# A decoder kernel in which rounded fp32 halves give way to plain fp32 products, and the experts' second products move behind the next first ones

## What is computed

```python
for l in range(4):
    h = rmsnorm(x, sg[l])
    x = attn_block(h, h, sWq[l], sWk[l], sWv[l], sWo[l], sbo[l], pe_q, pe_q, mask) + x
    h = rmsnorm(x, cg[l])
    x = attn_block(h, chunked_seq, cWq[l], cWk[l], cWv[l], cWo[l], cbo[l], pe_q, pe_k, None) + x
    h = rmsnorm(x, fg[l])
    x = gelu(h @ fW1[l] + fb1[l]) @ fW2[l] + fb2[l] + x
# attn_block: 8 heads of 64, rotary embedding of q and k, softmax(q k^T) v, @ Wo
h = relu(einsum('bth,ehf->betf', x, W1) + b1);  y = einsum('betf,efh->beth', h, W2)   # MoE
y = silu(xf @ wg[e].T) * (xf @ wu[e].T) @ w_down[e].T                                 # GLU
```

## Time and profile before

| | us |
|---|---|
| median of three runs | 1341.22 (1340.53 to 1349.2) |
| span of the profiled execution, first to last instruction | 1334.7 |
| median of the runs less this span | 6.5 |
| PE busy | 1161.6 (87%) |
| DVE, ACT, POOL busy | 779.1, 706.8, 554.6 |

### The profile page before, as it was taken

One profiled execution on the slowest core, in us unless ns is written; L12 is line 12 of the kernel. 1 busy time (PEld: TensorE's weight loads), 2 busy tenths in 40 slices (PEclk: granted clock), 3 DMA queues, 4 the chain that ended last, 5 costly groups with the idle time before them and its releaser, 6 DMA issues.

```text
span 1334.7 us, 21229 instructions
## 1 busy us (share of the span) xinstructions
PE 1161.6 (87%) x7374; PEld 766.2 (57%) x7374; DVE 779.1 (58%) x2164; ACT 706.8 (53%) x1889; POOL 554.6 (42%) x643
## 2 busy tenths in 40 slices
PE   4399998979999897999988899988669976897898
PEld 2255564655556566565556555555559964454687
DVE  7766655476665557666555766565352235775455
ACT  2177665547766536767543776655144433563332
POOL 2467543467754347766236677433221010111110
PEclk8699999999999999999999999999879988998899
DMA  4001010001111000200100020100111100000010
GB/s 139 16 10 17 17 40 9 25 1 39 25 17 41 25 1 1 47 17 17 41 25 1 1 49 17 33 1 1 48 52 33 49 0 1 1 1 1 9 36 26
DMA packets 60857, 31.00 MB, mean 23 GB/s; under 512 B 34260, under 2 KB 52049, under 8 KB 60753
## 3 DMA queue, kind: packets, MB, share of 16 engines
q1 hardware_dynamic: 60753, 29.64, 8.6%
HBM read 28.47 MB, written 1.16 MB: 22 GB/s over the span
## 4 chain that ended last, share of the span: by engine, by line
PE 69%; DVE 13%; POOL 6%; DMA 6%; ACT 4%; issue 2%; SPq 0%; POOLq 0%; DVEq 0%
PE bank L1644 11%; PE bank L1598 7%; PE bank L1704 7%; PE bank L1621 7%; PE bank L1861 4%; DMA dram_r<-recs 4%; PE bank L2081 3%; PE bank L1672 3%; PE bank L1792 3%; PE bank L1794 2%; PE bank L1793 2%; PE bank L1655 2%; PE bank L1590 2%; DMA recT<-dram_r 2%; PE bank L1675 1%
## 5 line engine op out<-in xcount | busy, mean ns | idle before, releaser
L937 DVE CUSTOM_DVE_ANT_0 bank<-bank,maskrow 128x512 f32<-128x512 f32 x256 | 172.1, 715 | 96.2 <-PE bank L1598 95.0
L1343 ACT ACTIVATE probs<-bank,tops 128x512 f32<-128x512 f32 x256 | 174.3, 685 | 99.0 <-DVE tops L937 98.3
L1355 ACT ACTIVATE KA<-bank 128x512 f32<-128x512 f32 x256 | 139.0, 600 | 25.2 <-PE bank L1621 20.5
L1598 PE MATMUL bank<-QR 64*128 64x512 f32 x768 | 126.1, 436 | 16.7 <-DVE rot L926 12.1
L1621 PEld LDWEIGHTS bank<-ident,probs 128*128 128x128 f32 x1024 | 117.0, 141 | 38.6 <-issue 26.3
L1644 PE MATMUL bank<-KA,Vs 128*64 128x512 f32 x512 | 135.4, 615 | 3.9 <-DVE AT L960 3.9
L1621 PE MATMUL bank<-ident,probs 128*128 128x128 f32 x1024 | 134.3, 274 | 2.3 <-ACT Vs L1315 2.3
L1339 ACT ACTIVATE probs<-bank,tops 128x154 f32<-128x154 f32 x256 | 96.5, 387 | 67.9 <-DVE tops L934 66.8
L925 DVE TENSOR_TENSOR rot<-bank,cos 128x512 f32<-128x512 f32 (+1 forms) x112 | 73.5, 656 | 63.8 <-PE bank L1675 54.6
L1598 PEld LDWEIGHTS bank<-QR 64*128 64x128 f32 x768 | 65.2, 189 | 44.2 <-issue 24.2
L703 POOL TENSOR_TENSOR rot<-rot,sin 128x512 f32<-128x512 f32 x48 | 61.2, 1276 | 61.9 <-DVE rot L926 61.9
(11 more groups left out here) (274 smaller groups left out, 2545.8 us busy)
## 6 DMA issues: line engine op xcount, KB each, us to landing
recT<-dram_r SPq DMA_DIRECT2D x56, 128.0 KB, 3.3
W<-in_W SPq DMA_DIRECT2D x8, 256.0 KB, 3.1
Vc<-in_wup SPq DMA_DIRECT2D x8, 192.0 KB, 2.4
W<-in_sWk SPq DMA_DIRECT2D x4, 256.0 KB, 4.2
W<-in_sWq SPq DMA_DIRECT2D x4, 256.0 KB, 4.4
W<-in_sWv SPq DMA_DIRECT2D x4, 256.0 KB, 4.7
wo<-in_sWo SPq DMA_DIRECT2D x4, 256.0 KB, 3.8
ck<-in_cWk SPq DMA_DIRECT2D x4, 256.0 KB, 2.8
```

The costliest lines, as they stand in the source:

```text
L937: v.tensor_tensor_reduce(bank[i][:, :], bank[i][:, :], maskrow[:, u.b * S:(u.b + 1) * S], -SCALE, 3.0e38, ALU.add, ALU.min, tops[:, g % 4, ...
L1343: c.activation(to, bank[i][:, :], ACT.Exp, bias=tops[:, g % 4, e, 0:1], scale=-1.0, accum_out=sums[:, n, e, k:k + 1]).then_inc(q.probs_rea ...
L1355: c.activation(turned_self(u)[:, half, :, k * P:(k + 1) * P], bank[4 + half][:, :].rearrange("p (c t) -> p c t", t=P), ACT.Copy).then_inc( ...
L1598: ins = mm(bank[first + e][:, :], QH[rows_of(e), u.j, a, w], KH[rows_of(e), u.j, c, :], start=(n == 0), stop=(n == 2))
```

## The change

All halves go. The five weight matrices are used as loaded, the input is `hT` alone, rotated keys and queries are one tile each (`rope_sum` in place of `rope_halves` and `rope_alone`), and each former triple is one plain fp32 product. The copies and subtractions on ACT, DVE and POOL go with them, also the store of x to DRAM and its reload, which had made room for halves. In both expert blocks the second products of b = 1 come behind the first products of b = 0 of the next expert, and the weights of the first and of the second product have loads and semaphores of their own. The diff, cut:

```diff
-                    for n, (a, c) in enumerate(((0, 0), (0, 1), (1, 0))):
-                        for e in range(2):
-                            ins = mm(bank[first + e][:, :], QH[rows_of(e), u.j, a, w], KH[rows_of(e), u.j, c, :],
-                                     start=(n == 0), stop=(n == 2))
+                    for e in range(2):
+                        mm(bank[first + e][:, :], QT[rows_of(e), u.j, c0:c0 + P], KT[rows_of(e), u.j, u.b * S:(u.b + 1) * S],
+                           start=True, stop=True).then_inc(q.scores_full, 1)
...
-                mm(bank[i][:, :], whigh[name][:, w], inh[:, S0], start=True, stop=False)
-                mm(bank[i][:, :], wlow[name][:, w], inh[:, S0], start=False, stop=False)
-                pe.wait_ge(q.low_ready, low_at[b])
-                return mm(bank[i][:, :], whigh[name][:, w], inl[:, S0], start=False, stop=True)
+                return mm(bank[i][:, :], whole[name][:, w], hT[:, S0], start=True, stop=True)
...
-                    lend([i], q.low_ready)
-                    input_at[b], low_at[b] = see.next(q.hT_ready), see.now(q.low_ready)
+                    lend([i], q.hT_ready)
+                    input_at[b] = see.now(q.hT_ready)
...
-                elif p.what in ("k", "q") and p.b == 0 and p.j < 2:
-                    rope_alone()
                 elif p.what == "k":
-                    rope_halves(KH[:, p.j, :, :])
-                elif p.what == "q":
-                    rope_halves(QH[:, p.j, :, :])
-                elif p.what == "cq":
+                    rope_sum(KT[:, p.j, S0])
+                elif p.what in ("q", "cq"):
                     rope_sum(QT[:, p.j, S0])
...
-                if p.what == "k" and (p.b, p.j) == (0, 1):
-                    low_alone(KH, "k", p.l, 0)
-                elif p.what == "q" and (p.b, p.j) == (0, 1):
-                    low_alone(QH, "q", p.l, 0)
...
-                    by_parts(bank[2 + j][:, :], e % 2, slice(j * P, (j + 1) * P), b).then_inc(q.moe_up_full, 1)
+                    mm(bank[2 + j][:, :], ew1[e % 2][:, j * P:(j + 1) * P], hT_of(b), start=True,
+                       stop=True).then_inc(q.moe_up_full, 1)
...
+            expert_up(0, 0)
+            router(wr[:, 0, :])
             for e in range(E):
...
+                expert_up(e, 1)
...
-                for b in range(B):
-                    expert_down(e, b)
+                expert_down(e, 0)
+                if e + 1 < E:
+                    expert_up(e + 1, 0)
+                expert_down(e, 1)
...
             for e in range(2, E):
+                sp.wait_ge(q.moe_up_ready, 2 * F0CH * (e - 1))
+                load_expert0(e % 2, e)
                 sp.wait_ge(q.moe_down_full, 2 * (e - 1))
-                load_expert0(e % 2, e)
+                load_second0(e % 2, e)
```

More of the change, by code:

```diff
@@ L167 @@
 ORDER = Order()
[L170 to L176, removed]
 def biases(l):
@@ L772, in layers @@
                         piece(p)
-                    if step.unit:
-                        parts(step.unit.l, step.g % 48)
-            def low_weights(to, w, high):
-                pool.wait_ge(q.split_high, see.next(q.split_high))
-                g.tensor_tensor(to, w, high, ALU.subtract).then_inc(q.split_ready, 1)
-            def low_inputs(after):
-                for b in range(B):
-                    w = slice(b * S, (b + 1) * S)
-                    pool.wait_ge(q.hT_ready, after + b + 1)
-                    g.tensor_tensor(hTl[:, w], hT[:, w], hTh[:, w], ALU.subtract).then_inc(q.split_ready, 1)
             def norm_powers():
@@ L808, in _ @@
             layers()
-            low_weights(wl[0], ew1[0][:, :], wh[0])
             norm_powers()
-            low_inputs(INPUTS["moe"])
-            for e in range(1, E):
-                low_weights(wl[e % 2], ew1[e % 2][:, :], wh[e % 2])
             norm_powers()
@@ L1315, in values @@
                 c.activation(dst, src, ACT.Copy).then_inc(q.v_ready, 1)
-            def halved_inputs():
-                for b in range(B):
-                    act.wait_ge(q.hT_full, see.n["hT_full"] + 1)
-                    c.activation(hTh[:, b * S:(b + 1) * S], bank[6 + b][:, :], ACT.Copy)
-                    input_of(b, 6 + b, 1.0)
             def logits_out(bias):
@@ L1360, in spread_out @@
                 c.activation(recT[:, u.n % 2, :], bank[7][:, :], ACT.Copy).then_inc(q.spread_ready, 1)
-            def round_alone(part, what, l, j):
-                act.wait_ge(q.alone_sum, see.next(q.alone_sum))
-                c.activation(part[:, j, 0, :], rot[:, (ORDER.made[what, l, 0, j] - 1) % 2, 0, :],
-                             ACT.Copy).then_inc(q.alone_high, 1)
             def piece(p):
@@ L1378, in piece @@
                     values(Vc[0:n, p.j, :], bank[p.bank][0:n, :])
-                elif p.what == "k" and (p.b, p.j) == (0, 1):
-                    round_alone(KH, "k", p.l, 0)
-                elif p.what == "q" and (p.b, p.j) == (0, 1):
-                    round_alone(QH, "q", p.l, 0)
                 elif p.what == "first":
@@ L2086, in _ @@
             inputs()
+            slots = [e % 2 for e in range(E)] + [2]
+            glu_up(0, 0, 0)
+            router(wr[:, 1, :])
             for e in range(E + 1):
-                n = e % 2 if e < E else 2
-                for b in range(B):
-                    glu_up(e, n, b)
-                    if e == 0 and b == 0:
-                        router(wr[:, 1, :])
-                    if e == 0 and b == 1:
-                        logits_turn()
-                for b in range(B):
-                    glu_down(e, n, b)
+                glu_up(e, slots[e], 1)
+                if e == 0:
+                    logits_turn()
+                glu_down(e, slots[e], 0)
+                if e < E:
+                    glu_up(e + 1, slots[e + 1], 0)
+                glu_down(e, slots[e], 1)
 def kernel(**inputs):
```

189 lines of the change are left out of this document (42 added, 147 removed).

## The result

The changed kernel takes 1357.6 us (median of 4 runs, 1354.5 to 1358.5), the kernel before 1342.2 (median of 4, 1340.5 to 1349.2): +15.4 us, a ratio of 1.0117 with a 95% interval of 1.0079 to 1.0154. I had forecast 1378, with a range of 1360 to 1394.

What follows compares the result with a forecast made beforehand. The prediction took PE to bound layers and experts (busy 87% of the span); 71.6 us of dearer products less 33.1 of gains gave +38.5, from the median 1341.2 to 1379.7, taken as 1378 for upward rounding, range 1360 to 1394.

Steps and rivals of the forecast that it cites:

- Projection +0.16, scores +0.165: Layers: a plain projection costs 0.16 us more, +25.6 in all; a pair of self scores 0.165 more, +21.
- rival 2: Self scores run one head after the other, +1.03 us per pair, 132 instead of 21 us: 1489; chance 0.03.
- Experts +25, heads -2.5: MoE and GLU: plain first products with two leads of 0.1 cost +25 us; ending first-product waits for POOL's low half gains 2.5.
- The wait for the low half, 9.4 + 0.8: Behind transposed inputs PE no longer waits for DVE's subtraction: 9.4 us gained in four layers, 0.8 at the last up.
- Between layers, 13.2 + 3.3: First scores start earlier as DVE embeds without waiting on rounding: 13.2 us gained between layers, 3.3 before the first.
- most of that penalty in: First scores of a layer, slow at 1.2 GHz after idle time, were forecast to stay mostly slow; 0.4 us gain allowed.
- The rule weighed: Between layers a shorter gap may keep the clock at 2.4 GHz, making the sum 3 us lower; not adopted.
- Waits for scaled values, 3.9: PE's 5 waits for row sums that went through DRAM vanish under longer self steps: 3.9 us gained.
- The sum put on the median: The +38.5 us was added to the median of 1341.2, which stood 6.5 above the profiled span of 1334.7: 1379.7.
- rival 1: Relief between layers and behind transposed inputs outweighs dearer products: 8 us faster, 1333, or half-way 1345; chances 0.03 and 0.05.
- Rival 4: Plain products at their lowest price: scores +0.12, clock up between layers, POOL's sum faster, more waits gone: 1364; chance 0.15.
- Rivals 3 and 5: 3: chain between layers does not shorten, 1388, chance 0.15. 5: 1 us wait per expert in reordered GLU, 1386, chance 0.05.

Runs made afterwards that it cites:

- the repeat: The changed kernel run once more, unaltered, on another chip beside the kernel before (1329.6 us there): 1356.4 us, ratio 1.0205.
- experiment 8: Changed kernel with three transposes of the normalised input one step earlier in the written order: 1352.3 us, ratio 1.0167 against the kernel before.
- experiment 4: Kernel before with only keys, queries and scores of each layer's first two units (b = 0) plain, the rest in halves: 1320.8 us, ratio 0.9867.
- experiment 5: Changed kernel with unread stand-in ACT copies and DVE subtractions putting back DVE's wait ahead of its next embedding: 1372.5 us, ratio 1.0251 against the kernel before.
- experiment 7: Kernel before, all in halves, with three transposes of the normalised input one step earlier in the written order: 1321.1 us, ratio 0.9885.

## Why the prediction was wrong, step by step

- **What bounds the kernel**: right. PE's work set the time in layers and experts, and 206 us less on the other engines bought only what waits they had caused.
- **Projection +0.16, scores +0.165**: right to 0.01 in the trace. The self stages, which hold most of both, cost 19.9 us where the steps and the waits gave 19.0. The bound of 1.92 per pair (rival 2) is ruled out: the two heads' plain scores run side by side.
- **Experts +25, heads -2.5**: too high by 5. The leads were 0.13 per expert too dear, 2 us. The rest is at the heads: the first products in the GLU take 4.8 us against 4.95 before, though they are dearer, as the clock rises sooner when the 1.27 of idle ahead of them is gone, and PE's stop ahead of the first second product is 0.7 shorter. In the repeat the GLU is 1.3 us longer than in this trace, so a part of the 5 is scatter.
- **The wait for the low half, 9.4 + 0.8**: right as a wait (experiment 8), but it was priced without the clock. In the cross stages 1.65 us of idle behind the second transposed input lowered the clock in three of four layers and 0.87 in none; three falls less, at 1.3 to 1.7 us each, are most or all of the 4.7 us that the cross stages came out below the forecast.
- **Between layers, 13.2 + 3.3**: this step failed, and experiment 4 shows it best: without the dearer projections the term, less the scores there, gives 7.4 us in the four stretches, and 14.0 came. Its first half was right: the first scores start 2.6 us earlier after the second transposed input (12.02 us before, 9.45 after), where I had 2.4. But I left "most of that penalty in". In two of the three stretches the first scores take 1.99 us for 8 instructions, as above, and in the other 2.50, where the forecast wanted all near the low level; the down product behind them gains too. The two stretches are 25.73 us and the third 27.34, a difference of 1.6 by the clock alone; in the repeat on the other chip all three are at 25.7. Ahead of the first layer the first scores start 2.2 us earlier, as forecast (2.3), but from them to the end of the stretch it takes 0.9 us less instead of some 1.5 more: the clock fell there too before (2.93 us for the first 12 scores, now 1.99 for 8), and PE's wait of 0.80 for values ahead of the context keys is gone. With that the four stretches came out 4.1 us below the ledger.
- **The rule weighed**: the trace agrees with the Trainium skill (TensorE: Matmul & The Clock Gate, Part 1) against my choice, in two of the three stretches between layers (1.97 us of idle, and the clock stays up) and in all three of the repeat. I had put the rule at 3 us; it gave 3.2 between layers and some 4 more in the cross stages, which I hadn't asked about at all.
- **Waits for scaled values, 3.9**: 3.2 of them went, so the term held on the traced execution. Taken as fixed, it was wrong: the same wait is 3.4 and 8.9 us in other kernels with halves on that chip.
- **The sum put on the median**: wrong, by 5 to 6 us. The span of one execution was at the low end of a kernel that scatters by 1%, and the waits for scaled values, which differ between its relatives' traces, are among those that the change takes away. The error of 23.1 us (38.5 less 15.4) is thus 16.4 on the span and 6.7 by the choice of base. Of the 16.4 the clock and the first layer's wait have some 9 (4.1 and 4.7 above), the experts 5. Against the +27 of the other chip the sum is 12 too high.
- **Rivals**: rival 1 (relief outweighs) was the direction of the error. The last of my tests, "if the busy time of PE rises as said and the time does not, the relief was undervalued", is what the trace shows: +58.5 us busy, +22.1 in span. For the layers alone it came true: 46.6 us of dearer products, and a ratio of 1.0006. Rival 4 (lowest price, 1364) named the clock between layers, but gave it 3 us, and its cheaper scores are not there. Rivals 3 and 5 didn't appear. Two small sums of the forecast are off, and nothing hangs on them: rivals 3 and 5 together come to 1396, not 1394, and the room in the GLU loop is 3.5 - 2.7 = 0.8 us, not 0.5.

What stays open: 1.4 us at the start and 1.1 in the decaying attention, which I put down to the spread of single executions; and how the 16.4 us split to the last one or two.

## What to carry to other kernels

A wait on the bounding engine costs its length and, where the granted clock falls behind it, here 1.3 to 1.7 us more in the steps that follow, whether the wait was 1.65 or 4 us: ask of each wait that a change shortens what the rows behind it run at now. Before adding a sum to the median, look at how far the profiled execution lies from it and which waits make the runs differ. And when a change pays in one place and charges in many, do the paying part alone: here two units plain and three transposes moved give 27 us, where the whole change loses 15 to 27.

## What the runs showed of the hardware

- The same code on three chips: the kernel before took 1338.5 and 1336.6 us (two series) on one, and 1329.6 on each of two others; the changed kernel 1356.4 on one of the latter and, with the old order of the experts, 1357.3 on the first.
- POOL's sum of two tiles took 1.27 us alone and 1.59 or 1.60 while DVE subtracted from two tiles in SBUF (experiment 5, and 1.61 in the earlier trace rows), and DVE's subtractions took 1.08 to 1.50. The Trainium skill (SBUF — State Buffer, Who interferes with whom) says that a VectorE instruction with two SBUF inputs contends with GpSimd's reads, and the rows agree on the contention: in experiment 5 the subtraction of 1.08 us overlapped the sum's first 0.47 us, and the sum took 0.32 longer.
- A pair of plain scores on 64 rows each costs 1.06 us for four instructions of 512 columns, as much as two instructions of the full array (0.86) and 0.2.
- PE's granted clock fell to 1.2 GHz behind 3 of the 8 idle times of 1.65 to 1.66 us ahead of a cross stage's first products, behind 3 of 4 of 1.71 us in either kernel, behind none of 0.87, and behind one of three of 1.97 us between layers of the changed kernel (experiment 7). Each fall cost 1.3 to 1.7 us.
